# Reordering four instruction streams of a two-stage transformer kernel: normed tile before the division, projection before the turning, roots before the gelus, a high half before a table load

## The reference, cut to what matters

```python
def _layer(x, ...):                       # twice in each ffn block
    h = shift_token(x)
    q, k, v = split(h @ wqkv)             # 8 heads of 64
    q = l2norm(q) * qs; k = l2norm(k) * ksc
    q, k = rotary_xpos(q, k)
    o = local_attention(q, k, v)          # windows of 64: own and past window
    x = x + o @ wo
    h = layernorm(shift_token(x)) @ w1 + b1
    a, g = split(h)
    x = x + (a * gelu(g, approximate=False)) @ w2 + b2
...
x = x + attention(layernorm(x))
x = x + ffn(layernorm(x))
x = x + weighted_values(layernorm(x))
x = x + ffn(layernorm(x))
```

## Time and profile before

| | |
|---|---|
| median of 3 runs | 1581.75 us (1580.46 to 1586.36) |
| the profiled execution | 1587.68 us, span 1585.8 us |
| TensorE matmul busy | 1431.8 us (90%) |
| TensorE weight load busy | 1120.9 us (71%) |
| VectorE busy | 1356.6 us (86%) |
| ScalarE busy | 1227.6 us (77%) |
| GpSimd busy | 894.4 us (56%) |
| mean granted TensorE clock | 0.977 of full speed |

### The profile page before, as it was taken

How to read it: one execution, slowest core, us unless ns; L and a number is a source line. 1 busy time by engine, 2 the same in 40 slices (tenths; PEclk the granted TensorE clock), 3 DMA queues, 4 the chain that set the end, 5 groups by cost and what they waited for, 6 DMA issues and landing times.

```text
span 1585.8 us, 46462 instructions
## 1 busy us (share of the span) xinstructions
PE 1431.8 (90%) x18975; PEld 1120.9 (71%) x18975; DVE 1356.6 (86%) x1692; ACT 1227.6 (77%) x1834; POOL 894.4 (56%) x626
## 2 busy tenths in 40 slices
PE   5999997899999999999998757899999999999998
PEld 3777874777777777777776444677777777777776
DVE  6777757889999999999995866999999999999994
ACT  4876867678888888888885757688888888888884
POOL 3333005666666666676661645666666666766761
PEclk9999998999999999999999878999999999999999
DMA  4313003665665656657651003656656566665652
GB/s 120 107 47 97 4 7 72 126 120 118 114 125 121 121 115 123 121 116 122 128 96 28 0 7 69 128 123 120 121 123 120 118 120 123 119 122 122 115 103 73
DMA packets 359855, 157.46 MB, mean 99 GB/s; under 512 B 299410, under 2 KB 335836, under 8 KB 359644
## 3 DMA queue, kind: packets, MB, share of 16 engines
q1 hardware_dynamic: 359644, 154.51, 49.3%
HBM read 27.29 MB, written 6.29 MB: 21 GB/s over the span
## 4 chain that ended last, share of the span: by engine, by line
DVE 33%; ACT 23%; PE 19%; issue 11%; DMA 5%; POOL 5%; SPq 4%; DVEq 0%; ACTq 0%; POOLq 0%
DVE t L1270 9%; DMA t<-t 5%; POOL t L1436 4%; DVE t L1277 4%; DVE t L1289 4%; ACT t L1072 4%; DVE t L1254 3%; ACT t L1143 3%; PE PS L199 3%; PE PS L201 2%; DVE t L1323 2%; PE PS L200 2%; ACT t L1059 2%; ACT L1196 2%; ACT L1143 2%
## 5 line engine op out<-in xcount | busy, mean ns | idle before, releaser
L1430 POOL TENSOR_TENSOR t<-t 128x1024 f32<-128x1024 f32 x128 | 309.1, 2415 | 235.6 <-DVE t L1260 233.5
L1436 POOL TENSOR_TENSOR t<-t 128x512 f32<-128x512 f32 x256 | 319.5, 1270 | 147.8 <-DVE t L1270 147.5
L1270 DVE TENSOR_TENSOR t<-t 128x1024 f32<-128x1024 f32 x128 | 277.8, 2171 | 0.1
L1059 ACT ACTIVATE t<-PS 128x1024 f32<-128x1024 f32 x128 | 131.9, 1031 | 71.7 <-PE PS L201 71.6
L1277 DVE TENSOR_TENSOR t<-t,PS 128x1024 bf16<-128x1024 f32 x128 | 155.8, 1217 | 36.9 <-ACT PS L1079 36.9
L852 PE MATMUL PS<-t 128*64 128x65 f32 x4096 | 148.4, 225 | 41.9 <-DVE t L1323 40.0
L199 PE MATMUL PS<-wqh,HH 128*128 128x512 f32 x384 | 167.3, 436 | 18.6 <-DVE t L1260 16.0
L852 PEld LDWEIGHTS PS<-t 128*64 128x64 f32 x4096 | 130.6, 138 | 58.5 <-DVE t L1323 49.5
L1072 ACT CAST t<-t 128x1024 bf16<-128x1024 f32 x128 | 133.4, 1042 | 42.4 <-POOL t L1436 42.2
L1289 DVE TENSOR_REDUCE t<-PS 128x8 bf16<-128x1024 f32 x128 | 155.6, 1216 | 10.9 <-PE PS L801 10.9
L1254 DVE TENSOR_REDUCE t<-t 128x16 f32<-128x1024 f32 x128 | 154.3, 1206 | 7.5 <-ACT t L1059 7.4
(11 more groups left out here) (242 smaller groups left out, 3389.6 us busy)
## 6 DMA issues: line engine op xcount, KB each, us to landing
t<-t SPq DMA_DIRECT2D x254, 130.0 KB, 2.3
t<-turns SPq DMA_DIRECT2D x128, 128.0 KB, 2.8
t<-yT SPq DMA_DIRECT2D x108, 128.0 KB, 2.3
t<-t SPq DMA_TRANSPOSE x304, 3.3
t<-in_c_rope SPq DMA_DIRECT2D x32, 128.0 KB, 2.2
turns<-t SPq DMA_DIRECT2D x32, 128.0 KB, 2.1
t<-in_L_attn_a_x SPq DMA_DIRECT2D x4, 512.0 KB, 6.7
t<-yT SPq DMA_DIRECT2D x16, 127.8 KB, 3.2
```

The costliest lines, as they stand in the source:

```text
L1270: e.e.tensor_tensor(BL.ta[i % 2].rearrange("p (x h) d -> p x h d", x=2), BL.qn.rearrange("p (x h) d -> p x h d", x=2), cos.to_broadcast([1 ...
L1430: e.e.tensor_tensor(BL.tc.rearrange("p (x h) d -> p x h d", x=2), BL.qn.rearrange("p (x h) d -> p x h d", x=2), sin.to_broadcast([128, 2, ...
L1436: e.e.tensor_tensor(tv[:, :, 32 * s:32 * s + 32], tv[:, :, 32 * s:32 * s + 32], BL.tc[:, :, 32 * (1 - s):32 * (1 - s) + 32], ALU.add).then ...
```

## The change

Four pieces of code are written in another order. No instruction is added or removed, and no size or buffer changes.

1. VectorE: `normed(s - 1)` now stands ahead of `divide(s - 4)`.
2. TensorE: `project(s)` now stands ahead of `turn_result(s - 4)` and `feed_bank_6(s)`.
3. ScalarE: in step G the roots of tile s stand ahead of the three gelus and their table load, and the `gate` of that step stands behind the squares.
4. ScalarE: `high` and `high_there` of tile s-1, which belong to step G+1, stand in step G between the gelus and the table load behind them.

```diff
 # layers_pe
                 if on(3):
                     scores(s - 3)
                     take_off_maxima(s - 3)
+                if on(0):
+                    project(s)
                 if on(4):
                     turn_result(s - 4)
                 feed_bank_6(s)
-                if on(0):
-                    project(s)
 # layers_act
-                if on(2):
+                if on(2) and chunk_at(s, 13) is None:
                     high(s - 2)
-                if on(2):
                     high_there(s - 2)
...
-                if chunk_at(s, 12) is not None:
-                    gate(chunk_at(s, 12), 2, 6)
                 if on(0):
                     squares(s)
                 if s == 0:
                     norm(range(7, 8))
+                if chunk_at(s, 12) is not None:
+                    gate(chunk_at(s, 12), 2, 6)
...
+                if on(0):
+                    rnorms(s)
                 if chunk_at(s, 12) is not None:
                     gelus(chunk_at(s, 12), range(3))
+                    if on(1):
+                        high(s - 1)
+                        high_there(s - 1)
                     e.e.preload_act_table_set("natural_log_exp_and_others")
-                if on(0):
-                    rnorms(s)
 # layers_dve
+                if on(1):
+                    normed(s - 1)
                 if on(4):
                     divide(s - 4)
-                if on(1):
-                    normed(s - 1)
                 if on(2):
                     low(s - 2)
```

## The result

The changed kernel takes 1572.53 us (median of 11 runs), the kernel before 1581.84 us in the same comparison: ratio 0.9947, with a 95% interval of 0.9934 to 0.9959. It is faster by 0.5%, by 9 us where 36 were forecast: above the forecast of 1546 us, and outside the stated range of 1530 to 1566. Its profiled execution has a span of 1569.9 us.

A forecast was written before the change was run, and what follows sets the result against it. TensorE's own work (34.93 us of a 36.50 us period) was the floor, with waits for VectorE's chain above it. 28 periods x 1.05 = 29.4 plus 6.7 us made 36 off 1581.75: 1546 us, range 1530 to 1566.

The forecast's parts named there:

- What bounds the kernel, and the shadow: VectorE's chain runs through GpSimd's product plus a 1.08 us tail; low half and its 0.72 us wait are free behind it.
- Division behind the normed tile, 0.84 us off VectorE's chain: On VectorE the division moves into GpSimd's shadow, with 0.59 us to spare, shortening the chain by 0.84 us each step.
- That is the floor: no order gets a period below it: TensorE's own work in a four-step period, 36.50 less 1.57 us of waits, is 34.93 us whatever the order.
- It does not wait, by 0.14 us: TensorE reaches the projection 2.56 us behind the gather; its banks are free at 2.42, so no wait.
- That is not on the chain of the period: I count nothing: ScalarE squares the projection after copying the turned result; the squares hardly come earlier, and no effect on the period is counted.
- Cost 0.1 us a period: ScalarE's new order in G starts G+1's exponentials 4.1 us behind the gather, before 3.94, costing 0.1 us a period.
- So it protects the first part and gives nothing by itself.: ScalarE's reordering spares G+1 roots 0.6 us too late and a low half 0.2 us outside the shadow; no gain alone.
- The sum for a period: Gain 0.59 (G+1) + 0.58 (G+2) - 0.1 = 1.05 us, 35.45 for 36.50; bounds 0.5 to 1.57.
- How often: The second table load stands 28 times in the trace, so 28 periods of 1.05 us: 29.4 us (14 to 44).
- The steps ahead of the feed-forward: VectorE's chain holds steps before the feed-forward joins; 7.99 becomes 7.15 us, saving 6.7 us (5 to 8.4).
- The slower one: Rival: TensorE stands ahead of the projection for a late normed tile, some 120 steps; 0.5 us each gives 1606 us; chance 0.07.
- The transposes: Rival: waits for transposes replace VectorE's waits on TensorE, leaving a gain of 19 us, 1563 us; chance 0.16.

The follow-up runs named there:

- x2: Parts 3 and 4 alone (ScalarE's new order), TensorE and VectorE as in the kernel before: 1600.43 us, ratio 1.0127 to the kernel before.
- w1: Kernel before with only the turning moved between what feeds bank 6 and the projection, splitting the long products: 1587.58 us, ratio 1.0038 to the kernel before.
- y1: Changed kernel with ScalarE's squares put ahead of the copy of the turned result: 1561.76 us, ratio 0.9879 to the kernel before.
- x1: Parts 1 and 2 alone (VectorE's and TensorE's new order), ScalarE as in the kernel before: 1593.61 us, ratio 1.0082 to the kernel before.
- x5: Changed kernel with part 4 alone undone, the high half of G+1 behind the second table load again: 1582.61 us, ratio 1.0006 to the kernel before.
- w2: Changed kernel with squares ahead of the copy (except in G+1) and, in G+1, maxima reduced ahead of the addition: 1551.58 us, ratio 0.9812 to the kernel before.
- x4: Part 2 alone (projection ahead of the turning), VectorE and ScalarE as in the kernel before: 1655.80 us, ratio 1.0485 to the kernel before.

## Why the prediction was wrong

In one sentence: the waits that the change aimed at went away as forecast, but the prediction held TensorE's own work fixed at 34.93 us a period, put the squares' later place on ScalarE at nothing, and sized the waits for the normed tile and for the exponentials too small; of the 1.05 us a period that were forecast 0.29 are left. Point by point, by its steps:

- *What bounds the kernel, and the shadow.* Right. The rotation ends 1.08 us behind GpSimd in every kernel; shortening VectorE's largest wait by itself gave nothing (x2: 0.26 us sooner, and the rotation's product 0.23 longer). The sign that this product would take up to 2.5 us in G+1 did not come, and did not follow from my own sum: with 3.10 us of work ahead of it and GpSimd's end at 3.69 it takes 0.59 + 1.08 = 1.67 us, as measured.
- *Division behind the normed tile, 0.84 us off VectorE's chain.* Right: L1262 follows the maxima by 1.14 us, the division kept its time beside GpSimd, and the gather that ends G+1 no longer waits.
- *"That is the floor: no order gets a period below it", 34.93 us of TensorE's own work.* This step failed, as far as it was used as the same number after the change. The order of TensorE's work is part of its length. One more group of long products behind short ones costs 0.06 to 0.07 us a step (w1). It counts in G, G+3 and G+1, which TensorE holds, some 0.2 us a period; in G+2, where the gather waits for VectorE, it is covered.
- *"It does not wait, by 0.14 us", projection against the normed tile.* Failed in G and G+2: 0.08 and 0.18 us. I had the reduction of the maxima start 0.12 us behind the gather everywhere in this check, but 0.3 behind the gather that begins G+2 in the sum for the period. It was 0.32 (576.13 to 576.45), so G+2 had no margin; yet G+2 is held by VectorE, so its 0.18 us lengthen the period only through the later squares. In G VectorE was within 0.05 us of its forecast; what was missing is the 0.15 us from the normed tile's end to the projection's start, which I had put at nothing.
- *"That is not on the chain of the period: I count nothing", the squares behind the copy of the turned result.* This step failed, and it is the largest. The copy waited 0.91 us for the turning behind the projection, the squares came behind it, and the sums waited for the squares. The rotation ended 6.03 us behind the gather in G (562.99 - 556.96), as forecast, and the sums stood 0.21 behind it. In G+2 the same made 8.96 us of the forecast 8.65, and y1, which undoes only this order, gives 8.65. In all y1 gains 0.38 us a period, 11 us in the median.
- *ScalarE in G, "Cost 0.1 us a period".* Mis-sized: TensorE stood 0.3 us in G+1 for the exponentials. They started 4.37 us behind the gather, beyond the 4.3 that I had named as a sign of being wrong. y1 takes 0.13 us off G+1; the rest of the 0.2 that I missed remains.
- *"So it protects the first part and gives nothing by itself."* Right in kind, far too low in size: without ScalarE's part the kernel is slower than before (x1), and without part 4 alone the gain is gone (x5). The roots were late by 1.0 us in x1 and not by 0.6.
- *The sum for a period.* Forecast 35.45, measured 36.21 to 36.24, about 0.8 more. By steps: G 0.14 (0.07 for the extra group, 0.08 behind the normed tile), G+3 0.07 (the extra group), G+1 0.27 (0.07 for the extra group, 0.2 of the 0.3 for the exponentials), G+2 0.31 (the sums behind the squares). The first three are TensorE's; the last is VectorE's chain.
- *"How often", 28 times.* The two traces hold 26 whole periods, and from the first G to the last they gave only 2.9 and 2.1 us in the two calls, 5.0 for the forecast 29.4. Part of that loss is the first G+1 of each call, 0.9 and 1.4 us longer than before: there TensorE stands 1.9 us for the exponentials in the first call. No second product (L914) lies in the step ahead of it; that this is why ScalarE's chain shows there was not tried.
- *The steps ahead of the feed-forward.* Forecast 6.7 us (5 to 8.4) from VectorE's chain, 7.99 to 7.15 us a step. Between the first gather and the first G the two calls gave 5.1 and 3.6 us, 8.7 in all. The size came out near, and by luck: where TensorE stood for VectorE's normed tile the gathers were 7.32 us apart before (283.17 to 290.49) and 7.41 in the changed kernel (280.17 to 287.58). The gain came in steps where TensorE had stood for transposes or for VectorE's `scaled`, such as 10.74 us (306.84 to 317.58) which became 8.33 (303.92 to 312.25).
- *Spans and medians.* The spans of the two profiled executions differ by 16 us and the medians by 9; the profiled execution of the kernel before, 1587.68 us, is slower than all 11 timed ones (1579.2 to 1586.4), so the medians are the better measure of the whole and the rows of where it lies.
- *The rivals.* The slower one was in the right place: TensorE does stand ahead of the projection. At 0.26 us in four steps it is a fifth of what would decide, and 0.18 of that lies in the step that VectorE holds. x1 shows the decisive form: with late roots it wins. The transposes did not take the place of VectorE's waits in the changed kernel (2.3 us in the stretch, before 3.9); they begin to where the period falls to 35.3 (w2).

Open: why the first long product behind short ones takes 0.08 us longer. The weight load that starts only 0.03 us ahead of it is seen; that it is the cause was not tried by itself. G is 10.05 to 10.07 us in the faster versions; 9.88, the extra group and the 0.08 behind the normed tile, which is there too, make 10.02 or 10.03, and the last 0.02 to 0.05 were not taken apart.

## What to carry to other kernels

When a stream is reordered to take a stall off the critical path, write down for every engine when each of its instructions gets its input and when it is now reached, in every step of the pattern and not in one: here three engines were within 0.1 to 0.3 us of each other, and a term that one step hides is a stall in the next. Moving an instruction ahead on one engine asks for the same move on the engine that reads it (projection ahead of turning wants squares ahead of the copy; that one swap gave 11 us, about as much as the whole change). And the work of a full engine is not a constant: count how often its order goes from short products to long ones.

## What the runs showed that I had not expected

- The first 512-column product behind 128-column ones takes 0.31 us from start to start, the following 0.23; one more such place in each step cost 0.06 to 0.07 us a step (w1: 36.65 for 36.52 us a period, ratio 1.0038).
- Waits of 0.08 to 0.3 us on TensorE appear in no bracket of idle time; they show only in the starts of the following rows, since a product's modelled end covers them. The busy time of TensorE grew by 13 us for the same products, in the period shown from 34.93 to 35.63; these waits and the extra first products are both in it.
- Edits were far from additive: parts 1 and 2 alone +12 us, parts 3 and 4 alone +19, all four -9 by the medians.
- The projection that waits for two semaphores starts 0.15 us behind the end of the last one's producer, the one that waits for a single one 0.05 to 0.06 (G against G+1 and G+2, and all steps of x4). That the second semaphore is the cause was not tried by itself.
- High halves of G+1 that start 1.4 us later (2.34 us behind the gather for 0.93) cost 0.04 us in quiet periods and up to 3.3 us in others (x5).
